# Two GAT layers in a graph network kernel: where ScalarE issues a group's merged exponential

## The reference, cut to what matters

```
def gat_layer(x, src, dst, W, a_s, a_d, b, concat):
    h = (x @ W).reshape(N, H, C)
    alpha_s = einsum('nhc,hc->nh', h, a_s)
    alpha_d = einsum('nhc,hc->nh', h, a_d)
    logits = leaky_relu(alpha_s[src] + alpha_d[dst], 0.2)
    m = segment_max(logits, dst)
    e = exp(logits - m[dst])
    s = segment_sum(e, dst)
    a = e / s[dst]
    out = segment_sum(h[src] * a[:, :, None], dst)
    out = out.reshape(N, H * C) if concat else out.mean(axis=1)
    return out + b

h   = gat_layer(x, src, dst, W1, as1, ad1, b1, concat=True)
out = gat_layer(h, src, dst, W2, as2, ad2, b2, concat=False)
x   = layernorm(x + out)
```

## Time and profile before

| what | value |
|---|---|
| median of three runs | 3666.76 us |
| the profiled execution | 3672.33 us |
| its span, first to last instruction | 3670.4 us |
| granted TensorE clock, mean | 0.608 |
| VectorE busy | 2254.0 us, 61% |
| GpSimd busy | 2331.2 us, 64% |
| TensorE busy | 1199.0 us, 33% |
| ScalarE busy | 1189.2 us, 32% |
| first GAT layer, about | 1206 to 1622 us of the span |
| second GAT layer, about | 1626 to 1985 us of the span |

### The profile page before, as it was taken

One profiled execution on the slowest core, in us unless ns is written; L12 is line 12 of the kernel. 1 busy time (PEld: TensorE's weight loads), 2 busy tenths in 40 slices (PEclk: granted clock), 3 DMA queues, 4 the chain that ended last, 5 costly groups with the idle time before them and its releaser, 6 DMA issues. The chain is left out here.

```text
span 3670.4 us, 33500 instructions
## 1 busy us (share of the span) xinstructions
PE 1199.0 (33%) x5638; PEld 886.2 (24%) x5638; DVE 2254.0 (61%) x4835; ACT 1189.2 (32%) x3433; POOL 2331.2 (64%) x2220
## 2 busy tenths in 40 slices
PE   0555565570122254633553000000000008974221
PEld 0444444450122133421221000000000006763221
DVE  4877777616676767758986333336874425558553
ACT  0666666420222245413553222221000006462110
POOL 5777777777772677127740777774037767751777
PEclk9877777655555555556876555555555557586555
DMA  1777777641111244324652555552000028782000
GB/s 47 210 218 220 218 217 223 189 131 25 42 47 40 57 121 114 116 64 120 195 166 82 147 149 153 154 148 83 0 8 20 20 56 228 196 239 74 18 18 17
DMA packets 247009, 420.84 MB, mean 115 GB/s; under 512 B 75747, under 2 KB 83251, under 8 KB 245677
## 3 DMA queue, kind: packets, MB, share of 16 engines
q1 hardware_dynamic: 176014, 354.96, 31.9%
q0 software_dynamic: 70912, 65.07, 8.6%
HBM read 185.19 MB, written 236.81 MB: 115 GB/s over the span
## 5 line engine op out<-in xcount | busy, mean ns | idle before, releaser
L230 POOL DMA_INDIRECT edge_rows<-x_rows,norm_s x400 | 430.5, 1076 | 141.2 <-issue 121.3
L804 PE MATMUL banks<-ident,cross_in 125*65 125x125 f32 (+4 forms) x26 | 11.2, 430 | 1139.3 <-DVE cross_in L827 746.7
L246 POOL DMA_INDIRECT out_dram<-n_out,scat_i x200 | 222.7, 1113 | 157.8 <-DVE n_out L2155 95.8
L246 POOL DMA_INDIRECT x_rows<-r_x,src_scat_i x200 | 223.1, 1115 | 125.4 <-DVE r_x L2049 63.4
L804 PEld LDWEIGHTS banks<-ident,cross_in 125*65 125x65 f32 (+4 forms) x26 | 3.9, 150 | 1144.9 <-DVE cross_in L827 749.2
L634 DVE TENSOR_REDUCE n_var<-n_sq 125x8 f32<-125x512 f32 x125 | 85.6, 686 | 304.6 <-ACT n_sq L648 304.6
L230 POOL DMA_INDIRECT edge_rows<-in_x_dram,dst_i x200 | 220.6, 1103 | 61.0 <-issue 61.0
L246 POOL DMA_INDIRECT norm_rows<-edge_rows,scat_i x200 | 209.0, 1045 | 67.7 <-issue 64.4
L230 POOL DMA_INDIRECT tops<-norm_rows,src_i x200 | 207.0, 1035 | 69.8 <-issue 67.4
L230 POOL DMA_INDIRECT edge_rows<-h_rows,norm_s x200 | 203.8, 1019 | 70.5 <-issue 60.7
L230 POOL DMA_INDIRECT edge_rows<-x_rows,key_i x200 | 199.2, 996 | 77.4 <-issue 60.7
(11 more groups left out here) (455 smaller groups left out, 4807.6 us busy)
## 6 DMA issues: line engine op xcount, KB each, us to landing
h_rows<-r_h SPq DMA_DIRECT2D x125, 462.0 KB
x_rows<-r_x SPq DMA_DIRECT2D x125, 241.5 KB
x_rows<-r_x SPq DMA_DIRECT2D x125, 224.0 KB
r_x<-x_rows SPq DMA_DIRECT2D x125, 224.0 KB
x_rows<-n_out SPq DMA_DIRECT2D x125, 224.0 KB
n_in<-in_x_dram SPq DMA_DIRECT2D x100, 224.0 KB
x_mixed_edge_rows<-e_dup SPq DMA_DIRECT2D x50, 448.0 KB
r_x<-x_rows SPq DMA_DIRECT2D x50, 241.5 KB
```

What stands on the lines that cost most here:

```text
L230: g.indirect_dma_start(out=to[:, j, :], out_offset=None, in_=table, in_offset=bass.IndirectOffsetOnAxis(ap=idx[:, j:j + 1], axis=0)).then_ ...
L246: g.indirect_dma_start(out=table, out_offset=bass.IndirectOffsetOnAxis(ap=idx[:, j:j + 1], axis=0), in_=frm[:, j, :] if len(frm.shape) == ...
L804: pe.transpose(crossings["bank"][0:cols, 0:rows], frm, ident[0:rows, 0:rows]).then_inc(s_tout, 1)
```

## The change

In both layers the call of `merged_act` moves up to stand directly behind `logits_act`. ScalarE then waits for the second set of arguments and issues the merged exponential ahead of the evictions and copies of the previous group's last chunks (layer one) or ahead of `norm_chunk(start - 1)` (layer two). Nothing is added or removed. In a layer's first group nothing stands between the two, so nothing changes there.

```diff
@@ -1764,11 +1764,11 @@
                 for n, (start, end) in enumerate(groups):
                     logits_act(act, s1, n)
+                    merged_act(act, s1, n)
                     if n:
                         turned_chunk(start - 1)
                         row_chunk(start - 2)
                         row_chunk(start - 1)
-                    merged_act(act, s1, n)
                     act.wait_ge(s1.exps, 2 * n + 2)
                     factors_act(act, s1, start, start)
                     act.wait_ge(s1.args, 3 * n + 3)
@@ -1931,9 +1931,9 @@
                 for n, (start, end) in enumerate(groups):
                     logits_act(act, s2, n)
+                    merged_act(act, s2, n)
                     if n:
                         norm_chunk(start - 1)
-                    merged_act(act, s2, n)
                     act.wait_ge(s2.exps, 2 * n + 2)
                     factors_act(act, s2, start, start)
                     act.wait_ge(s2.args, 3 * n + 3)
```

## The result

Over six runs each, the changed kernel takes 3634.75 us (3625.47 to 3645.39) against 3666.49 us (3650.98 to 3700.3), ratio 0.9886 with a 95% interval of 0.9854 to 0.9919. That is 1.1% faster, 42 us by the ratio (30 to 54), where 38.4 had been forecast. The medians alone stand 31.7 us apart, and the later one is 6.8 us above the 3628 of the forecast.

The account below looks back on a forecast made before the run. No engine is full; VectorE's 88.0 us of waits for the merged exponential at group boundaries lengthen the layers. Layer one 19.5 plus layer two 18.9 gives 38.4 us, from the 3666.76 median to 3628, range 3617 to 3648.

Parts of the forecast that it names:

- The ordinary boundary of layer one: Merge and first multiplications run under the evictions, then VectorE waits for factor copies: 4.49 us gained, less at narrower groups.
- The first boundary of layer one: Layer one's boundary before chunk 9's group: 3.54 us gained alone, 2.2 kept because gathered rows arrive little earlier.
- the reach of the gathers: Layer one, first boundary: rows land about 1361.5, so at most 2.7 us kept; denser VectorE work takes off 0.5.
- The rival with TensorE's clock: Layer one boundaries: 2.4 GHz granted for two chunks' products, 12 to 18 us more gain, 3610 to 3616; chance 0.07.
- a shift of E by more than 1 us: Sign of being wrong: E, the end of the last eviction at a layer one boundary, was to stay put.
- Layer two: VectorE's five merged-exponential waits, 24.3 us, shrink to about 0.05 each; after corrections and gathers 18.9 us gained.
- the correction of 0.7: Layer two, chunk 19's and last boundaries: factor copies behind the root come late, costing 0.7 each, 1.4 us for both.
- 3.0 + 0.8 = 3.8 us: Layer two gains not kept because gathered rows bind: 3.0 at the first boundary, 0.8 at the second.
- Saved table loads: Layer two: ScalarE's table loads fall by ten; what that saves elsewhere is hidden and booked at nothing.
- a drain beside the load: Layer two: skill page's drain of about 1.38 us per table switch, sum some 2.8 us smaller; not taken.
- doing little: Rival: VectorE's wait is replaced at nearly full length by another; 0 to 25 us gained, 3642 to 3667; chance 0.13.
- slower row loads: Rival, layer two: ScalarE's 42.2 us of waits for heads rows surface, 3.8 us slower, 3671; chance 0.03.

Follow-up runs that it names:

- e9: Full change, plus factor copies ahead of the evictions (layer two: norm_chunk) and layer one's own-row scaling ahead of the last eviction: 3620.03 us against 3683.33, ratio 0.9831.
- e5: The changed kernel again, on a chip where the kernel before takes 5503.3 us: 5457.41 us, ratio 0.9917.
- e10: The changed kernel again, on a chip where the kernel before takes 3683.33 us: 3630.74 us, ratio 0.9882.
- e8: Changed kernel plus unused identity products on TensorE in layer one, 6 behind each chunk within a group, 20 at group ends: 5444.93 us, ratio 0.9896 to the kernel before.
- e3: Kernel before, with layer one's merged exponential moved between the evictions of the last two chunks, layer two unchanged: 5464.15 us against 5487.89, ratio 0.9945.
- e6: Changed kernel with the factor copies also ahead of the evictions (layer one) and norm_chunk (layer two): 5440.69 us, ratio 0.9888 to the kernel before.
- e4: Changed kernel plus a one-column exponential behind layer two's factor copies, bringing ten table loads back: 5453.91 us, ratio 0.9932 to the kernel before.

## Why the prediction was right, step by step

**The ordinary boundary of layer one**, 4.49 us: right in mechanism and size. Where TensorE stays at 1.2 GHz the full groups take 64.85 and 60.55 us (4.3), on the other chips 64.31 and 59.86 (4.45). The group of chunk 19 takes 55.13 and 50.86 there (4.27; forecast 4.29), the last 53.54 and 49.63 on the first chip (3.91; forecast 3.98). The covered ScalarE delay was 0.9 us and cost nothing. That the wait comes back as one for the factor copies of about 8.8 us is what the trace shows (8.81).

**The first boundary of layer one**: forecast 3.54 alone and 2.2 kept. Measured 60.58 - 56.99 = 3.6, all of it kept. The step that failed is the reach of the gathers: the rows of chunks 9 to 13 were there at 1366.56 without a wait, 57.0 us after those of the group before; the forecast had taken 57.9 as their distance plus 0.5. The last gathers of the two groups, after:

```profile
1307.04 0.95 POOL L230 DMA_INDIRECT edge_rows<-x_rows,norm_s  x1 [0.31 <-issue]
...
1363.82 1.16 POOL L230 DMA_INDIRECT edge_rows<-x_rows,norm_s  x1 [0.30 <-issue]
```

They are 56.8 us apart, before 57.9, so denser VectorE work did not delay this stretch of gathers; the 0.5 us taken off for it had the wrong sign here. VectorE started 2.74 us behind the second of them, and the first had landed 2.53 us after its start: the gain fitted with about 0.2 us to spare, which is luck. Taken from one execution, such a landing time isn't good to a microsecond. In e9, where VectorE worked with fewer pauses still, the same two gathers are 58.55 us apart, and VectorE waited 8.05 us, so the term is real and was only sized too large for this change.

**The rival with TensorE's clock** was given 0.07 and is partly true. It moved the last eviction forward by 1.6 us at chunk 14 in the profiled execution (group 58.64 instead of 60.55) and by 0.7 at chunk 19. The prediction had named a shift of E by more than 1 us as a sign of being wrong, and at chunk 14 that sign appeared. Other traces of the same kernel show it at other boundaries: 55.49 at chunk 14 in e5, 58.52 at chunk 9 in e10. "What precedes the boundary is unchanged" was the argument against it. It doesn't hold: the idle time behind each boundary is shorter, so TensorE's work stands otherwise at the next one, and the eight unchanged boundaries had no such case where ten of twenty changed ones had. In e8 TensorE had more work, and the granted clock was 0.66 to 1.00. That the shorter idle time is the reason in the changed kernel itself is argued, not shown; that the same boundary gets different clocks in different executions, and that e3 and e6 had no case at their boundaries, shows that the change alone doesn't decide it.

**Layer two**, 18.9 us: the layer gained 20.75 us from its second group's start and lost 0.85 in front of it, 19.9. The sum fits, the single steps less well.

- Chunk 14's group gave 5.4 us, for a stall of 5.68 before. Chunk 19's gave 5.8 (forecast 6.28 less 0.05 and the correction of 0.7, so 5.5).
- The correction wasn't needed at chunk 19, because TensorE's sum of the last chunk ran at the higher clock (4.46 instead of 6.83 us). At the last boundary that sum took 6.2 us in both traces, and the copies were late by 0.62 us, as the correction says.
- The last group gave only 3.6 us, for a stall of 5.94. It lost 1.7 us again to the wait for the layer's last squares, 3.88 us before and 5.56 after. The forecast has no such term. The reason is TensorE's clock once more; its last sum, first before, then after:

```profile
1970.20:1974.80 4.60, 4.54 (x10) 1.77 (x10) 1.30 (x3) 0.38 (x3) 0.00 (x0) 1.00 0.36 111
```

```profile
1931.70:1938.00 6.30, 6.22 (x10) 2.38 (x10) 1.36 (x3) 0.00 (x0) 0.00 (x0) 0.73 0.26 81
```

- For the gathers the forecast gave up 3.0 + 0.8 = 3.8 us and expected the wait at chunk 9 to grow by 3. It fell from 1.77 to 0.90 us; a wait of 1.59 came at chunk 14 instead, where there had been none. In all, VectorE's wait for rows went from 4.5 to 6.1 us, 1.6 more, in e10 from 4.5 to 8.9, 4.4 more. So the mechanism is right, its place wasn't, and the size lies within what executions differ by.

**Saved table loads**, booked at nothing: at most 1.6 us in e4. Nothing speaks for a drain beside the load: at chunk 19 of layer two 1.30 us lie between the starts of load and root also here.

**The sum.** From the second groups' starts, layer one gave 22.9 us instead of 19.5, layer two 20.75. With the longer waits for rows at those starts (1.3 and 0.85 us) it is 21.6 and 19.9, 41.5 in the trace; by the ratio it is 42 (30 to 54), by the medians 31.7. Layer one's excess over the forecast is the gathers' term (1.4 us) and the clock's (1.7 at chunk 14 and 0.6 at chunk 19). In layer two the clock took 1.7 us back. That the total came out within 4 us is in part luck: terms of this size went both ways, and the interval of the ratio is too wide to test them. What tests the mechanism is the groups' lengths and the waits. The rivals of doing little and of slower row loads fell: heads rows delay ScalarE by 48.3 us in 12 places (42.2 before), but no new wait inside groups came of it.

## What to carry to other kernels

An engine's wait that is taken away is worth the work that can then run ahead of the next thing it needs, and no more. Here 4.3 to 4.5 of 13.4 us, because the next two needed things (factor copies, own rows) stood behind the same evictions; moving all three gave three times as much (64.3 to 51.0 us per full group), as long as the rows were there. Within an in-order queue, first list what the waiting engine needs next and where each stands, then put work into the queue's own idle gaps. Then ask which supplier comes next: once VectorE waited for nothing, it ran into the row gathers.

## What the runs showed of the hardware that was not expected

- TensorE's granted clock at the same place of the same kernel differs between executions. Over the products of chunk 14's boundary it was 0.50 in e10, 0.61 in the first trace of the changed kernel and 0.86 in e5, and the same 46 instructions were busy for 13.64, 12.00 and 9.22 us.
- That reaches VectorE through ScalarE: its wait for layer two's last squares is 3.88 us with the ten instructions before it at 1.00, and 5.56 us with them at 0.73.
- The eight runs on the two slower chips took 5404 to 5477 us; the two kernels among them that also ran elsewhere take 3620 and 3631 us there. In layer one's first group there, ScalarE's instructions stand 1.4 us apart with "issue" as the cause, where they follow each other within 0.25 us elsewhere (16 in 3.93 us). From e5:

```profile
2148.25 0.35 ACT L1745 ACTIVATE e_dup<-r_x,tops 125x64 f32<-125x64 f32 x1 [1.04 <-issue]
...
2149.65 0.35 ACT L1745 ACTIVATE e_dup<-r_x,tops 125x64 f32<-125x64 f32 x1 [1.05 <-issue]
2151.05 0.35 ACT L1745 ACTIVATE e_dup<-r_x,tops 125x64 f32<-125x64 f32 x1 [1.05 <-issue]
```

What holds the issue back wasn't tried. From the third group on layer one's groups are only some 0.6 us shorter than on the first chip, where TensorE's clock is the same (59.89 and 60.55).
